# A four-layer transformer kernel on one core: batch 0's share of the last mixture layer's first steps moved into the last two blocks of the linear attention

## What is computed

```
x = layernorm(x + L1_attn(x))     # linear attention: 32 heads of 64
x = layernorm(x + L1_ffn(x))      # mixture of experts and shared product

# L1_attn
q = relu(h @ Wq); k = relu(h @ Wk); v = h @ Wv
kv = einsum('bhsd,bhse->bhde', k, v)
normalizer = clip(einsum('bhsd,bhd->bhs', q, k.sum(axis=2)), 1e-6, None)
out = (einsum('bhsd,bhde->bhse', q, kv) / normalizer[..., None]) @ Wo + bo

# L1_ffn: 64 experts, 6 chosen by each token, 32 tokens at most for each expert
logits = x @ gate_w.T; scores = softmax(logits); topk_w, topk_i = top_k(scores, 6)
y = sum over the chosen experts of topk_w * (silu(x @ w_gate) * (x @ w_up)) @ w_down
shared = silu(x @ sw_gate) * (x @ sw_up) @ sw_down
return y + shared
```

## Time and profile before

| | |
|---|---|
| median of 3 runs | 1489.11 us (1487.36 to 1490.24) |
| the profiled execution's own time | 1489.89 us |
| its span in the trace | 1488.1 us |
| PE busy in the span | 1402.1 us (94%) |
| DVE, ACT, POOL busy | 934.1, 577.7, 555.8 us |
| block 15 and the end of its loop | about 1258.8 to 1281.6 us |
| from there to the first expert group's product | to about 1356 us |

### The profile page before, as it was taken

One profiled execution on the slowest core, in us unless ns is written; L12 is line 12 of the kernel. 1 busy time (PEld: TensorE's weight loads), 2 busy tenths in 40 slices (PEclk: granted clock), 3 DMA queues, 4 the chain that ended last, 5 costly groups with the idle time before them and its releaser, 6 DMA issues.

```text
span 1488.1 us, 23868 instructions
## 1 busy us (share of the span) xinstructions
PE 1402.1 (94%) x8118; PEld 1119.1 (75%) x8118; DVE 934.1 (63%) x2158; ACT 577.7 (39%) x1457; POOL 555.8 (37%) x483
## 2 busy tenths in 40 slices
PE   9999999999999999899999999999999999788990
PEld 7777777777777777677777688788788788665650
DVE  5777777777777777773443466565665665676113
ACT  4444444444444444542122243343343333342322
POOL 3655555555555555300014122523523522204223
PEclk9999999999999999999999999999999999899986
DMA  5000000000002000110000110200200001957984
GB/s 180 1 11 1 12 0 11 0 11 0 11 0 65 8 0 0 21 65 0 1 0 1 41 39 15 72 8 16 71 7 14 8 8 44 272 179 224 279 230 127
DMA packets 68221, 76.39 MB, mean 51 GB/s; under 512 B 14205, under 2 KB 55445, under 8 KB 68149
## 3 DMA queue, kind: packets, MB, share of 16 engines
q1 hardware_dynamic: 56517, 58.36, 13.6%
q10 hardware_dynamic: 8560, 12.36, 2.7%
q0 software_dynamic: 3072, 4.72, 1.6%
HBM read 66.22 MB, written 9.21 MB: 51 GB/s over the span
## 4 chain that ended last, share of the span: by engine, by line
PE 81%; DVE 7%; POOL 4%; ACT 2%; issue 2%; DMA 2%; SPq 1%; POOLq 0%; ACTq 0%; DVEq 0%
PE ps L1683 37%; PE ps L1822 9%; PE ps L1796 7%; PE ps L1784 5%; PE ps L1859 4%; PE ps L1950 4%; PE ps L1789 2%; PE ps L2164 2%; PE ps L2033 2%; PE ps L2229 1%; DMA wo<-in_L_attn_wo_dram 1%; PE ps L2023 1%; PE ps L2246 1%; PE ps L1824 1%; PE ps L1786 1%
## 5 line engine op out<-in xcount | busy, mean ns | idle before, releaser
L793 ACT ACTIVATE probs<-ps,nm 128x128 f32<-128x128 f32 (+3 forms) x256 | 134.0, 526 | 149.9 <-DVE nm L1174 149.8
L636 POOL TENSOR_TENSOR qk<-q,ksb 128x512 f32<-128x512 f32 x64 | 83.4, 1303 | 284.0 <-ACT q L888 212.2
L1822 PE MATMUL ps<-kT,qT 128*128 128x128 f32 (+3 forms) x512 | 174.5, 449 | 4.6 <-ACT probs L793 4.6
L1089 DVE TENSOR_TENSOR pT_low<-ps,pT 128x384 fp32r<-128x384 f32 (+2 forms) x256 | 99.5, 449 | 123.1 <-ACT pT L719 121.9
L1106 DVE TENSOR_TENSOR prod<-ps,rope_sb 128x1024 f32<-128x1024 f32 x128 | 149.9, 1211 | 7.3 <-PE ps L1683 7.3
L719 ACT ACTIVATE pT<-ps 128x384 fp32r<-128x384 f32 (+2 forms) x256 | 84.8, 416 | 152.6 <-PE ps L1859 152.6
L514 POOL TENSOR_TENSOR qT<-prod 64x512 f32<-64x512 f32 x64 | 81.2, 1269 | 167.5 <-DVE prod L1106 128.9
L1796 PE MATMUL ps<-U,oT 128*128 (+1 forms) x512 | 124.5, 386 | 0.0
L514 POOL TENSOR_TENSOR kT<-prod 64x512 f32<-64x512 f32 x64 | 81.4, 1272 | 108.7 <-DVE prod L1106 106.2
L1174 DVE TENSOR_REDUCE nm<-ps 128x1 f32<-128x128 f32 (+3 forms) x256 | 113.2, 481 | 9.4 <-PE ps L1824 9.4
L1231 DVE SCALAR_TENSOR_TENSOR acc<-ps,rinv,acc 128x256 f32<-128x256 f32 x256 | 109.4, 478 | 12.0 <-PE ps L1796 12.0
(11 more groups left out here) (263 smaller groups left out, 2774.0 us busy)
## 6 DMA issues: line engine op xcount, KB each, us to landing
eg<-in_L_ffn_w_gate_dram SPq DMA_DIRECT2D x16, 704.0 KB
eg<-in_L_ffn_w_up_dram SPq DMA_DIRECT2D x16, 704.0 KB
ed<-in_L_ffn_w_down_dram ACTq DMA_DIRECT2D x10, 640.0 KB
ksb<-ks_dram SPq DMA_DIRECT2D x16, 256.0 KB, 3.3
ed<-in_L_ffn_w_down_dram SPq DMA_DIRECT2D x6, 640.0 KB
rows_dram<-rows ACTq DMA_DIRECT2D x4, 640.0 KB, 3.3
acc<-in_L_attn_x_dram SPq DMA_DIRECT2D x4, 512.0 KB
wq_in<-in_L_attn_wq_dram SPq DMA_DIRECT2D x8, 256.0 KB, 2.9
```

What stands on the lines that cost most here:

```text
L636: nc.gpsimd.tensor_tensor(qk[:], q3[:], ksb[b % 2][:], ALU.mult).then_inc(qk_ready, 1)
L793: nc.scalar.activation(probs[hh][:, off:off + (i + 1) * P], ps[:, BS + i % 2, 0:(i + 1) * P], ACT.Exp, bias=nm[:, hh, i:i + 1], accum_out= ...
L1089: return nc.vector.tensor_tensor(o, whole, hi.bitcast(F32), ALU.subtract)
L1822: pe.matmul(ps[:, bank, 0:(i + 1) * P], qT[:, hh, b, i * P:(i + 1) * P], kT[:, hh, b, 0:(i + 1) * P], start=True, stop=False)
```

## The change

It does for batch 0, inside blocks 14 and 15, what stood behind block 15:

- SP: the five loads of the shared weights are issued after the key sums of block 14 (before: after those of block 15), and the key sums of block 15 after them.
- At the end of block 14: PE turns gw_in (2 transposes) ahead of `grams`; ACT splits gwT and sw; DVE splits gwT, makes batch 0's rows and splits sw.
- Block 15, i = 0: PE `turn_x3(0)` into banks 1 and 5, ACT `x3_halves(0)`, DVE `x3_rests(0)`. Steps i = 2 and 3: PE makes half of `logits(0)` each, ahead of `turn`. POOL writes the table countdown (two instructions) in step i = 1; before it did so after the loop.
- Behind block 15: DVE `top_logits(0)` ahead of the last `turned`; PE `gate_up4(0, 0)` ahead of the last `outputs`; DVE takes `choose(0)` ahead of the last `add3`, and `x3_rests(1)` ahead of batch 3's statistics; ACT `gate4(0, 0)` ahead of `x3_halves(1)`.
- x3T and rows lie at other addresses, the functions named stand earlier in the text, and the waits on `consts4` have new counts. No instruction is added or taken away.

```diff
-        x3T = [[place(f"x3T{i}{h}", 32 + 8 * i + 4 * h, [P, KD, T], F32R) for h in range(2)] for i in range(3)]
-        rows = [place(f"rows{i}", at, [P, TPB, ROW]) for i, at in enumerate((56, 61, 85))]
+        x3T = [[place(f"x3T{i}{h}", 48 - 8 * i + 4 * h, [P, KD, T], F32R) for h in range(2)] for i in range(3)]
+        rows = [place(f"rows{i}", at, [P, TPB, ROW]) for i, at in enumerate((61, 56, 85))]
...
+        def x3_bank(b, k):
+            return (1, 5)[k] if b == 0 else k
...
-            for b in range(1, BATCH):
+            for b in range(1, BATCH - 1):
                 load_key_sums((CHUNKS - 1) * BATCH + b, b % 2)
-            sp.wait_ge(k_ready, 4 * BLOCKS)
+            sp.wait_ge(k_ready, 4 * BATCH * (CHUNKS - 1))
+            sp.wait_ge(wk3_ready, CHUNKS)
             for w, name in enumerate(("gate", "up")):
...
             sp.dma_start(gw_in[:], io["L1_ffn_gate_w"]).then_inc(sw_loaded, 16)
...
+            load_key_sums(BLOCKS - 1, (BATCH - 1) % 2)
...
+                        if b == 3 and i == 1 and last:
+                            pool.wait_ge(kv_ready, BLOCKS)
+                            pool.wait_ge(qk_ready, u + 1)
...
+                                iota(countdown[64 * h:64 * h + 64, :, :], [[-T, BATCH], [-1, 2 * P]], TOK - 2 * P * h)
...
+                        if last and b == 3 and i == 0:
+                            x3_halves(0)
...
+                        if i == 3 and last and b == 2:
+                            act.wait_ge(sw_loaded, 5 * 16)
+                            act.wait_ge(gw_turned, 1)
+                            copy(gwT[0][:], ps[:, 5, 0:KD * E1].rearrange("p (k e) -> p k e", k=KD)).then_inc(sw_hi, 1)
...
+                            act.wait_ge(q_ready, (BLOCKS - 1) * TPB)
+                            copy(sw[0][:], sw_in[:]).then_inc(sw_hi, 1)
...
-            x3_halves(0)
-            act.wait_ge(gw_turned, 1)
-            copy(gwT[0][:], ps[:, 2, 0:KD * E1].rearrange("p (k e) -> p k e", k=KD)).then_inc(sw_hi, 1)
-            act.wait_ge(sw_loaded, 5 * 16)
-
-            act.wait_ge(q_ready, BLOCKS * TPB)
-            copy(sw[0][:], sw_in[:]).then_inc(sw_hi, 1)
             exps4(0)
+            gate4(0, 0)
             x3_halves(1)
             store_rows(0)
-            gate4(0, 0)
             exps4(1)
...
+                        if i == 0 and last and b == 3:
+                            x3_rests(0)
...
+                        if last and b == 2 and i == 3:
+                            dve.wait_ge(sw_hi, 1)
+                            rest(gwT[1][:], ps[:, 5, 0:KD * E1].rearrange("p (k e) -> p k e", k=KD), gwT[0][:]).then_inc(sw_lo, 1)
+                            rows4(0)
+                            dve.wait_ge(sw_hi, 2)
+                            rest(sw[1][:], sw_in[:], sw[0][:]).then_inc(sw_lo, 1)
...
             add3(BLOCKS * TPB - 2, TILES - 2)
+            top_logits(0)
             turned(BLOCKS * TPB - 1)
...
-            rows4(0)
+            rows4(1)
+            choose(0)
             add3(BLOCKS * TPB - 1, TILES - 1)
+            x3_rests(1)
             dve.wait_ge(added3, BLOCKS * TPB)
             statistics16(BATCH - 1, acc)
-            x3_rests(0)
-            dve.wait_ge(sw_hi, 1)
-            rest(gwT[1][:], ps[:, 2, 0:KD * E1].rearrange("p (k e) -> p k e", k=KD), gwT[0][:]).then_inc(sw_lo, 1)
-            rows4(1)
-            top_logits(0)
-            dve.wait_ge(sw_hi, 2)
-            rest(sw[1][:], sw_in[:], sw[0][:]).then_inc(sw_lo, 1)
-            choose(0)
-            x3_rests(1)
             list_tokens(0)
             hidden4(0, 0)
...
+            def turn_x3(b):
+                pe.wait_ge(x3_ready, b * TPB + TPB)
...
+                for k in range(KD):
+                    if b == 0 and k == 1:
+
+                        pe.wait_ge(sw_lo, 1)
+                    for i in range(TPB):
+                        last = pe.transpose(ps[:, x3_bank(b, k), i * P:(i + 1) * P], rows[b % 3][:, i, k * P:(k + 1) * P], ident[:])
+                    last.then_inc(x3_turned, 1)
+
...
+                        if i == 0 and last and b == 3:
+                            turn_x3(0)
...
+                            if last and b == 3:
+
+                                pe.wait_ge(x3lo_ready, KD)
...
+                        if i >= 2 and last and b == 3:
+                            logits(0, (2 * i - 4, 2 * i - 3))
                         if not (start and i == 0):
                             turn(u - 1)
...
+                        if i == 3 and last and b == 2:
+                            pe.wait_ge(sw_loaded, 5 * 16)
+                            for k in range(KD):
+                                at_k = pe.transpose(ps[:, 5, k * E1:(k + 1) * E1], gw_in[:, k * P:(k + 1) * P], ident[0:E1, 0:E1])
+                            at_k.then_inc(gw_turned, 1)
...
+            pe.wait_ge(sw_lo, 2)
+            pe.wait_ge(added3, BLOCKS * TPB - 1)
+            gate_up4(0, 0)
+            outputs(BLOCKS * TPB - 1, BLOCKS - 1, TPB - 1)
             pe.wait_ge(q_copied, BLOCKS * TPB)
-            turn_x3(0)
-            outputs(BLOCKS * TPB - 1, BLOCKS - 1, TPB - 1)
-            pe.wait_ge(sw_loaded, 5 * 16)
-            for k in range(KD):
-                last = pe.transpose(ps[:, 2, k * E1:(k + 1) * E1], gw_in[:, k * P:(k + 1) * P], ident[0:E1, 0:E1])
-            last.then_inc(gw_turned, 1)
-            pe.wait_ge(added3, BLOCKS * TPB)
-            logits(0)
             turn_x3(1)
-            pe.wait_ge(sw_lo, 2)
-            gate_up4(0, 0)
             turn_marked(0)
             logits(1)
+            pe.wait_ge(added3, BLOCKS * TPB)
             gate_up4(0, 1)
             turn_x3(2)
             gate_up4(0, 2)
```

92 lines of the change are left out of this document (44 added, 48 removed).

## The result

The changed kernel takes 1478.19 us (median of 4 runs, 1477.65 to 1479.20), the kernel before, run beside it, 1488.40 us (4 runs, 1487.36 to 1490.24). The ratio is 0.9927 with a 95% interval of 0.9915 to 0.9939: 10.2 us faster. The prediction was 1479.6 us. The profiled execution of the changed kernel took 1477.78 us by its own time, with a span of 1475.9 us.

A forecast was written before the change was run, and what follows sets the result against it. Batch 0's serial chain of small steps behind block 15 was taken to bound the kernel. 3.5 us later in block 15, plus 9.4 us of chain, less the former 22.4, gives -9.5 us: 1479.6 us, range 1475 to 1485.

The forecast's parts named there:

- T2: Start of DVE's list for batch 0, at 1304.01 before; predicted 9.5 us earlier, at about 1294.5.
- G: Start of the first expert group's product, at 1356.06 before; predicted at about 1347.
- Block 14: Earlier loads and splits of shared weights there cost nothing; only PE's turn of gw_in adds 0.34 us.
- Block 15: Batch 0's turn and logits inside the loop delay the last linear-attention turn by 1.4 + 1.4 + 0.7 = 3.5 us.
- T1: End of the last turn of the linear attention, 1281.64 before; predicted 3.5 us later, at about 1285.1.
- From T1 to T2: From last linear-attention turn to batch 0's list: 9.4 us through PE, ACT, DVE and batch 3's statistics, against 22.4 before.
- Rival 1: PE's clock falls in the freed stretch behind the last turn: +4.3 us, some 1484 us; chance 0.15.
- 2, the clock stays up at the second shared product: At batch 0's `down4_products(0, 0)` half of 5.49 us goes: another -2.7 us, 1476.9 us; chance 0.10.
- 3, table switches that cost more than their rows: ACT's two table switches delay batch 1's split, so batch 0's list comes 2.4 us later, 1482 us; chance 0.02.
- 4, transfers alone: The experts' weight transfers alone set the end, so nothing is won: 1489 us; chance 0.06.
- 5, late stored rows: Batch 0's stored rows land late and hold up `rows4(3)` on DVE; slower, 1493 us with landing at 1324; chance 0.05.

The follow-up runs named there:

- e4: Changed kernel with POOL's two countdown table instructions moved from step 1 of block 15 to behind the small constants; 1486.34 us, ratio 0.9980.
- e6: Changed kernel with each half of batch 0's logits in the loop computed twice; 1483.37 us, ratio 0.9964.
- e5: Changed kernel with the shared weights' loads released by the keys of all 16 blocks instead of 12; 1486.36 us, ratio 0.9988.
- e2: Changed kernel with batch 0's whole logits behind the loop, ahead of its first shared product; 1480.59 us, ratio 0.9941.
- e3: Changed kernel with batch 0's first shared product behind batch 1's turn on PE, its activation behind batch 1's halves on ACT; 1478.49 us, ratio 0.9928.
- e8: Changed kernel with 20 unused identity turns on PE ahead of the second layer of batch 0's shared product; 1478.62 us, ratio 0.9928.
- e1: Changed kernel with batch 0's rows, turn, logits and first shared product back behind the loop, weights and tables staying moved; 1489.53 us, ratio 0.9998.
- e7: Changed kernel with batch 3's statistics moved from ahead of batch 0's list to ahead of batch 1's list; 1478.36 us, ratio 0.9927.
- e12: Changed kernel with the shared product behind batch 1's turn, statistics behind batch 0's list, filling turns ahead of second shared product and group 11; 1476.70 us, ratio 0.9906.

## Why the prediction was right, and where it was off

**The frame held.** The serial chain behind block 15 bounded the kernel, and lists that start earlier shift all behind them. Predicted: T2 9.5 us earlier, and the time as much. T2 came 9.57 us earlier, G 9.15 and the median 10.2. That 9.5 and 9.57 agree so closely is luck: seen from g, T2 came 10.62 us earlier, 10.3 with gw_in's turn, and the other 0.7 is what the two executions differ by ahead of the block. G came 10.2 us earlier from g, as much as the median. e4 and e6 move G by 5.4 and 2.6 us as seen from g, e5 moves it by 6.9, and the medians move by 8.2, 5.2 and 8.2 us (7.9, 5.5 and 9.1 by the ratios): nothing is swallowed behind G, and something is added (below).

**Block 14: nothing but gw_in's turn.** Confirmed: the turn is 0.34 us and stands at 1254.04. ACT still idles ahead of its copy of g, 1.18 us instead of 2.31:

```profile
1254.04 0.34 PE L2134 MATMUL ps<-ident,gw_in 64*128 64x64 f32 x2
...
1257.37 0.60 ACT L730 ACTIVATE g<-ps 128x512 f32<-128x512 f32 x1 [1.18 <-PE ps L1698]
```

**Block 15: 3.5 us predicted, 3.3 measured, of other parts.** From g on, T1 moved by 2.95 us (predicted 3.5 - 0.34 = 3.16), which is made of:

- up to the turn of tile 60: +0.88 (predicted 1.09 for `turn_x3(0)`);
- step 2, from the turn of tile 60 to that of 61: 3.93 to 4.97, +1.04 (predicted 1.42);
- step 3: 4.77 to 4.90, +0.13 (predicted 0.7). This term was mis-sized: I added the durations of PE's groups, 5.4 us, and of the four groups three start 0.17 to 0.24 us before the one ahead of them has ended. From the starts in the timeline, PE's own work in the step is 4.90 us. e6 shows the edge: from there on added work counts in full;
- the last step, where nothing was predicted: +0.51, and +0.39 in the turn itself. The clock fell there. In e2 to e5 it did not, after the same wait of 1.41 us, and there `outputs` took 1.69 or 1.70 us and the turn 0.66.

So the sum came out near for a reason that is partly luck: without the fallen clock (e3, whose edit stands behind T1) T1 is 2.0 us later from g and not 3.16, and the 0.9 us of the clock, which the forecast did not have there, made up for what it had counted too high.

**From T1 to T2: 9.4 predicted, 8.80 measured, by another way.** The table load, the exponentials and the second load ended 4.54 us after T1, as predicted (4.5). But `gate4`'s 0.60 us on ACT stands ahead of batch 1's copy, and that branch ended as late as PE's; the chain went through ACT. There are three ways, not two, and they end within some 0.3 us of each other: DVE's choice and `add3`, which the prediction let end earlier, are done at 1291.2, and batch 1's copy at 1291.3. The steps from batch 1's copy on (copy, DVE's rest, statistics) came out as summed. e3 frees PE's and ACT's at once and wins 0.2 us from T1 to T2, since DVE's stays.

**What was not named.** The placing of POOL's tables was costed right, at nothing (1271.21, 2.06 us, and the next qk behind it still waits 1.82 us). But the sum from T1 to T2 rests on it, and the prediction did not say so: without it the first list comes 3.6 us later and G 5.4 (e4; 4.7 and 6.4 from T1).

**The checks.** The list stands behind batch 3's statistics at 1294.44 (foretold 1294.5); the last turn ended at 1285.64 (1285.1); G is 1346.91 (1347). Two checks failed. The turns of tiles 61 and 62 were to stand 5.4 us apart and stand 4.90. And the clock was to be near 1.00 from 1284 to 1294, and it was 0.50 up to 1286. The prediction had called that a sign against itself; it cost about 1 us. Rival 1 had named the idle time around the last turn, but counted its cost only behind T1.

**The rivals.** *1, the clock falls in the freed stretch:* only at its beginning; from 1288 to 1310 it is 1.00. Its price was not summed rightly: 5.3 us at half rate are up to 5.3 more, not 4.3. *2, the clock stays up at the second shared product:* it fell again, with the same gap, and e8 prices it at 2.6 to 3.1 us:

```profile
1310.56 5.49 PE L2195 MATMUL ps<-swd,hid 118*128 118x256 f32 x12 [3.33 <-DVE hid L1517]
```

*3, table switches that cost more than their rows:* no. The load started at 1286.30, took 1.28 us and the exponential started at 1287.59; the second ended at 1290.18 and the SiLU started at 1290.19. Here the two switches stand on the path itself, so the extra 1.38 us each that the Trainium skill gives (ScalarE: Activation LUTs, What ACT_TABLE_LOAD costs) would be seen directly. By that page of the Trainium skill I estimate 11.6 us from T1 to T2 (8.80 and twice 1.38). It was 8.80. *4, transfers alone:* no, G moved with the lists. *5, late stored rows:* no. The stores were issued from 1291.08 and landed after 9.1 to 12.8 us; `rows4(3)` started at 1310.76, some 6 us after the last had landed (1292.14 + 12.8).

**Behind G, 2.8 us that the prediction did not have.** From the first to the last group's product it was 90.77 us before and 87.93 after, though nothing there was changed. All of it lies at two groups, 10 and 11. The kernel before:

```profile
1412.42 1.39 PE L2229 MATMUL ps<-eg,xsT 128*32 128x352 f32 x16
...
1421.98 2.58 PE L2229 MATMUL ps<-eg,xsT 128*32 128x352 f32 x16 [3.54 <-issue]
...
1433.45 0.80 PE L2229 MATMUL ps<-eg,xsT 128*32 128x352 f32 x8
```

```profile
1420.00:1432.00 12.00, 10.02 (x47) 5.64 (x48) 1.03 (x2) 0.70 (x2) 1.08 (x1) 0.57 1.09 303
```

and the changed one:

```profile
1403.25 1.39 PE L2255 MATMUL ps<-eg,xsT 128*32 128x352 f32 x16
...
1411.84 2.09 PE L2255 MATMUL ps<-eg,xsT 128*32 128x352 f32 x16 [2.57 <-issue]
...
1421.46 1.39 PE L2255 MATMUL ps<-eg,xsT 128*32 128x352 f32 x16 [0.97 <-issue]
```

```profile
1412.00:1416.00 4.00, 4.00 (x34) 1.34 (x26) 0.34 (x1) 0.70 (x2) 0.00 (x0) 0.57 1.10 282
```

PE waits ahead of group 11's product, 3.54 us before and 2.57 after (-0.97), and then works at the lower clock. The means of 0.57 over 12 us and over 4 us are 10.3 and 3.4 us at 0.50; before, 9.4 of them are behind the start of the product. From that product to the next it is 11.47 and 9.62 us (-1.85). Together -2.82. The profile names no releaser of these waits; by the code only the weights' transfers are left. The stretch from first to last product was 91 us in the traces of the kernel before, e1, e4 and e5, and 88 in those of the changed kernel, e2, e3, e6, e7, e8 and e12. It goes with how long the lower level lasts at group 11: some 10 us in the first four traces, 3.4 in the others, and none in e12. So the profiled execution of e4 (1485.31 us) lies 7.5 us above the changed kernel's, of which its later G gives 4.5 and this stretch 3.1. One kernel can take either: e6's seven times are 1480.55, 1480.78, 1481.82, then 1483.37, and 1485.18, 1485.61, 1485.67, and its trace, with 88 us, is that of the lowest. What makes it the one or the other I don't know: the idle time alone does not (3.54 us before and 3.55 in e7), and that it goes with the time at which the lists end is only argued. Nor does the median show it: it moved by 10.2 us, as G did from g.

**Open.** e3, e7 and e8 move G by 0.4, 0.7 and 3.0 us from T1 in their traces and their medians not at all. Executions of one kernel lie 1 to 6 us apart, 8 to 9 on the one chip, and one of e5's twelve, 1498.05 us at a mean clock of 0.934, lies 12 us above its median; one trace of each was taken, so I can't say whether their marks are the usual ones. The ratios' intervals are some 2 us either way, so the times can tell 5 us and not 1. Why the clock fell ahead of T1 in some executions is open. The 9 to 12 us on ACT on that one chip are open too.

## What to carry to other kernels

Where one batch's chain of small steps stands alone between two full stretches, take its first links into the loop ahead: in a step that a loop through another engine sets, they cost next to nothing up to the gap, and full price beyond it. Size that gap by the starts of the groups in the timeline, not by the sum of their durations. When one link is made shorter, look for every branch that meets behind it: here PE, ACT and DVE ended within 0.3 us of each other, and a swap that freed two of them won 0.2 us. And look for the small tables and constants that the shortened chain will want next: here they carried half of the gain or more, and left in their old place they would have taken it back (e4).

## What the runs showed of the hardware that was not expected

- The granted clock fell after a wait of 1.41 us in some executions (the changed kernel: 0.50 from 1284 to 1286) and not in others with the same wait (the kernel before and e1 to e5, `outputs` at 1.69 to 1.70 us).
- The idle time does not say how long the lower level lasts: at group 11 it lasted 10.3 us with 3.54 us idle (the kernel before) and 3.4 us with 2.57 (the changed kernel) and with 3.55 us idle (e7).
- Small products with no use kept the clock up in two gaps: with 2.40 us of them ahead of it the second shared product took 2.86 us instead of 5.49 (e8), and in e12 group 11's product took 1.39 instead of 2.09. The second won no time, since transfers set the pace there.
- On one chip ACT stood 9 to 12 us with its input there and no wait that the records name, in all three traces taken there. Both kernels were some 8 us slower on it and the ratio was unchanged (0.9926 against 0.9927).
